# Attention softmax sums inverted in columns and spread by a small product, with the written-out order of all engines laid anew

## What is computed

```python
attn = jax.nn.softmax(sim, axis=-1)
out = jnp.einsum('bhij,bhjd->bhid', attn, v)
out = out.transpose(0, 2, 1, 3).reshape(b, n, h * dh)
return out @ Wout
```

## Time and profile before

| | us |
|---|---|
| median of 3 runs | 3418.23 |
| lowest and highest | 3415.29, 3420.38 |
| the profiled execution's own time | 3428.19 |
| its span | 3425.9 |
| PE busy | 2829.8 (83%) |
| DVE busy | 2313.0 (68%) |
| POOL busy | 1460.9 (43%) |
| ACT busy | 1333.8 (39%) |

### The profile page before, as it was taken

The page is one execution under the profiler, slowest core; times in us unless marked ns, Lnnn a source line. Parts: engine busy times, 40 slices in busy tenths (PEclk is TensorE's granted clock), DMA queues, the critical chain, the costliest instruction groups (busy, mean ns, idle before and its releaser), DMA issues.

```text
span 3425.9 us, 47657 instructions
## 1 busy us (share of the span) xinstructions
PE 2829.8 (83%) x13729; PEld 1419.9 (41%) x13729; DVE 2313.0 (68%) x5792; ACT 1333.8 (39%) x2860; POOL 1460.9 (43%) x1765
## 2 busy tenths in 40 slices
PE   4788787888887877787888888888878788999999
PEld 3333333333333333333333333333333343666666
DVE  6767676768676878686767676767677776444443
ACT  3344434444444444444444343434344433111111
POOL 6354545444555454545454545454545453000000
PEclk8899998989898989898989898989999989999999
DMA  1000000000000000000000000000000010000000
GB/s 42 10 14 6 13 7 13 7 13 7 26 19 13 7 12 8 12 7 12 8 10 10 10 10 10 10 10 10 10 9 7 9 59 1 1 0 16 9 0 25
DMA packets 76232, 41.75 MB, mean 12 GB/s; under 512 B 19024, under 2 KB 74960, under 8 KB 75984
## 3 DMA queue, kind: packets, MB, share of 16 engines
q1 hardware_dynamic: 74448, 34.51, 3.8%
q0 software_dynamic: 1536, 4.20, 0.4%
HBM read 17.55 MB, written 4.19 MB: 6 GB/s over the span
## 4 chain that ended last, share of the span: by engine, by line
PE 39%; DVE 21%; POOL 19%; issue 17%; ACT 4%; POOLq 0%; DMA 0%; ACTq 0%; DVEq 0%
POOL acc L602 12%; PE ps L1188 7%; PE ps L1175 7%; DVE rl L897 5%; DVE ps L854 5%; PE ps L1056 5%; POOL rnorm L583 4%; PE ps L1127 4%; DVE tqk L827 4%; PE ps L1111 3%; DVE tqk L825 3%; PE ps L1084 3%; PE ps L1112 3%; PE ps L1053 2%; ACT probs L689 2%
## 5 line engine op out<-in xcount | busy, mean ns | idle before, releaser
L602 POOL TENSOR_TENSOR acc<-acc,probs 128x512 f32<-128x512 f32 (+4 forms) x944 | 897.0, 950 | 400.0 <-ACT probs L689 326.0
L689 ACT ACTIVATE probs<-ps,btab 128x512 f32<-128x512 f32 (+4 forms) x1408 | 761.9, 589 | 412.9 <-PE ps L1112 264.6
L1127 PE MATMUL ps<-probs,arena 128*64 128x512 f32 (+4 forms) x2816 | 652.4, 541 | 0.0
L854 DVE CUSTOM_DVE_ANT_0 ps<-ps,tab_l 128x512 f32<-128x512 f32 (+1 forms) x896 | 566.3, 672 | 101.4 <-PE ps L1084 98.9
L1111 PE MATMUL ps<-arena 128*128 128x512 f16 (+4 forms) x1408 | 504.4, 360 | 49.1 <-ACT probs L689 47.8
L1084 PE MATMUL ps<-arena 64*128 64x512 f16 (+4 forms) x1408 | 248.8, 346 | 306.4 <-DVE mx L854 300.6
L1112 PE MATMUL ps<-arena 128*128 128x512 f16 (+9 forms) x1408 | 495.8, 354 | 0.0
L580 POOL TENSOR_SCALAR nsq<-ssq 128x4 f32<-128x4 f32 (+1 forms) x272 | 74.6, 274 | 837.5 <-DVE ssq L814 836.8
L645 ACT ACTIVATE sq<-ps 128x256 f32<-128x256 f32 (+1 forms) x272 | 102.3, 376 | 733.2 <-PE ps L1056 731.2
L1056 PE MATMUL ps<-wqkv,xT 128*128 128x256 f32 (+1 forms) x1088 | 366.5, 471 | 0.0
L1084 PEld LDWEIGHTS ps<-arena 64*128 64x128 f16 x1408 | 74.9, 93 | 643.3 <-issue 640.0
(11 more groups left out here) (131 smaller groups left out, 3788.1 us busy)
## 6 DMA issues: line engine op xcount, KB each, us to landing
arena<-arena SPq DMA_DIRECT2D x512, 32.0 KB, 1.9
wqkv<-in_Wkv SPq DMA_DIRECT2D x32, 128.0 KB, 2.5
arena<-in_w SPq DMA_DIRECT2D x2, 2048.0 KB, 11.5
out<-h SPq DMA_DIRECT2D x8, 512.0 KB, 3.0
wqkv<-in_Wq SPq DMA_DIRECT2D x16, 128.0 KB, 2.4
arena<-augs SPq DMA_DIRECT2D x128, 1.0 KB
wo<-in_Wout SPq DMA_DIRECT2D x16, 128.0 KB, 2.2
h<-in_table,idx POOLq DMA_INDIRECT x32, 3.0
```

What stands on the lines that cost most here:

```text
L602: pool.tensor_tensor(a, probs[0:rows, (n - 2) % PB, 0:GW] if first else a, p, ALU.add).then_inc(sum_pool, 1)
L689: nc.scalar.activation(probs[0:rows, n % PB, 0:w], bank(S0 + n % 2)[0:rows, 0:w], ACT.Exp, bias=btab[0:rows, hh, z:z + 1]).then_inc(exp_do ...
L854: nc.vector.tensor_tensor_reduce(bank(A0 + hd)[:, 0:w], bank(A0 + hd)[:, 0:w], tab, 1.0, NEG, ALU.add, ALU.max, mx[:, hd, it, c:c + 1]).th ...
L1127: mm(bank(O0 + o % 2)[DH * hd:DH * hd + DH, c0:GW], vt[t % 2][0:rows, jt, hd, :], probs[0:rows, n % PB, 0:GW - c0], start=(jt == 0), stop= ...
```

## The change

1. The sums are no longer inverted as 128x512. ACT copies them from PSUM to `rl` (`keep_l`). Two DMAs on SP's queue bring one row of 512 for each head into `l_col`, 128 partitions x 4 for each head (`turn_l`). DVE inverts 128x8 (`inv_l`). Two DMAs bring the result back as two rows (`row_l`). PE multiplies these two rows with `of_head`, a 2x128 matrix of ones and zeros, which spreads them over 128x512 in a shared bank (`spread_l`).
2. ACT copies the output from its bank to `otf` (`keep_o`), which frees the bank. DVE multiplies it there with the spread inverses (`divide`). `wout` waits for that.
3. The planned times of nearly all entries are new. `turn_of` keeps entries that use the shared banks at least 0.9 slots apart. The stages of `project` have longer distances for pairs after the first (`LAGS`). `turn_shift` stands 4.4 slots behind `shift`, where it was 0.8. `wout` begins 7.7 slots behind `sums` and its pieces stand at least 2.4 slots apart (it was 2.7 and 2). `sums` stands 4.4 slots behind a group's last block (it was 2.6). `values` and `sum_p` stand later behind their exponentials.
4. `wsum` moves into a part of another buffer, and a wait on `var_ready` is added in `stats_of`.

```diff
+    def turn_of(time):
+        apart = 0.65 if time < 0 else 0.9
+        for other in sorted(taken):
+            if abs(other - time) < apart - 1e-6:
+                time = other + apart
+        taken.append(time)
+        return time
...
+    LAGS = [dict(square=0.4, ssq=1.2, inv=1.9, unit=3.2, high=3.5, low=4.3, turn=4.8),
+            dict(square=0.9, ssq=2.0, inv=2.3, unit=4.2, high=5.0, low=5.8, turn=7.0)]
...
-                at(s0 + 0.9, "shift", t, ig)
-                at(s0 + 1.7, "turn_shift", t, ig)
-                at(s0 + 2.3, "keep_shift", t, ig)
-                at(s0 + 2.4, "put_shift", t, ig)
+                at(s0 + 1.1, "shift", t, ig)
+                s1 = turn_of(s0 + 5.5)
+                at(s1, "turn_shift", t, ig)
+                at(s1 + 0.9, "keep_shift", t, ig)
+                at(s1 + 0.9 + 0.1, "put_shift", t, ig)
...
-            at(t0 + m - 0.9 * (m % 2) + 1.4, "sum_p", t, m)
-            at(t0 + (m | 1) + 1.9, "values", t, m)
+            at(t0 + m - 0.9 * (m % 2) + 1.85, "sum_p", t, m)
+            at(t0 + (m | 1) + 3.5, "values", t, m)
         for ig in range(NG):
-            e0 = t0 + 2 * last_block[ig] + 1
-            at(e0 + 2.6, "sums", t, ig)
-            at(e0 + 3.2, "divide", t, ig)
+            s0 = turn_of(t0 + 2 * last_block[ig] + 1 + 4.4)
+            sums_at[(t, ig)] = s0
+            at(s0, "sums", t, ig)
+            at(s0 + 0.9, "keep_l", t, ig)
+            at(s0 + 0.9 + 0.1, "turn_l", t, ig)
+            at(s0 + 2.9, "inv_l", t, ig)
+            at(s0 + 2.9 + 0.1, "row_l", t, ig)
+            at(s0 + 1.4, "keep_o", t, ig)
+            spread_at.append((turn_of(s0 + 5.0), t, ig))
...
+            def turn_l(t, ig):
+                o = NG * t + ig
+                sp.wait_ge(l_read, o + 1)
+                need(sp, li_out, 32 * o)
+                for hd in range(2):
+                    sp.dma_start(l_col[:, G * hd:G * hd + G], rl[DH * hd:DH * hd + 1, :]).then_inc(l_in, 16)
+
+            def row_l(t, ig):
+                o = NG * t + ig
+                sp.wait_ge(li_ready, o + 1)
+                for hd in range(2):
+                    sp.dma_start(rl[hd:hd + 1, :], l_col[:, G * hd:G * hd + G]).then_inc(li_out, 16)
...
+            def keep_o(t, ig):
+                o = NG * t + ig
+                act.wait_ge(pv_done, PAIR * t + 2 * last_block[ig] + 2)
+                need(act, w_ready, G * (o - 1))
+                nc.scalar.activation(otf[:, o % 2, :], bank(O0 + o % 2), ACT.Copy).then_inc(o_read, 1)
+
+            def keep_l(t, ig):
+                o = NG * t + ig
+                act.wait_ge(l_ready, o + 1)
+                need(act, rl_ready, o)
+                nc.scalar.activation(rl[:, :], shared_of("sums", t, ig)[:, :], ACT.Copy).then_inc(l_read, 1)
...
+            def inv_l(t, ig):
+                o = NG * t + ig
+                dve.wait_ge(l_in, 32 * (o + 1))
+                nc.vector.reciprocal(l_col[:, :], l_col[:, :]).then_inc(li_ready, 1)
+
             def divide(t, ig):
                 o = NG * t + ig
-                dve.wait_ge(l_ready, o + 1)
-                nc.vector.reciprocal(rl[:, :], shared_of("sums", t, ig)[:, :]).then_inc(rl_ready, 1)
                 dve.wait_ge(rl_ready, o + 1)
-                dve.wait_ge(pv_done, PAIR * t + 2 * last_block[ig] + 2)
-                need(dve, w_ready, G * (o - 1))
-                nc.vector.tensor_tensor(otf[:, o % 2, :], bank(O0 + o % 2), rl[:, :], ALU.mult).then_inc(o_read, 1)
+                dve.wait_ge(o_read, o + 1)
+                nc.vector.tensor_tensor(otf[:, o % 2, :], otf[:, o % 2, :], shared_of("spread_l", t, ig)[:, :], ALU.mult).then_inc(o_ready, 1)
...
+            def spread_l(t, ig):
+                o = NG * t + ig
+                pe.wait_ge(li_out, 32 * (o + 1))
+                z = shared_bank("spread_l", t, ig)
+                mm(bank(z)[:, :], of_head[:, :], rl[0:2, :], start=True, stop=True).then_inc(rl_ready, 1)
```

More of the change, by code:

```diff
@@ L194, in lm_tower_kernel @@
     at(-22, "null_unit")
-    at(-20, "null_turn")
-    at(-19, "null_keep")
+    s0 = turn_of(-20)
+    at(s0, "null_turn")
+    at(s0 + 0.6, "null_keep")
     at(-24, "zeros", 1)
-    project(0, -24, 1.6)
-    maxima(0, -14.4, 1.1, lambda g: -24 + 1.6 * (2 * g + 1) + 8)
+    project(0, -24, 1.7)
+    maxima(0, -14.4, 1.2)
+    t0 = max(shifts[(0, ig)] - 2 * blocks.index((ig, 0, 128, 0)) for ig in range(NG))
+    for t in range(PAIRS):
+        attend(t, t0 + PAIR * t)
+        at(t0 + PAIR * t - 40.0 if t else -16, "tables", t)
     for t in range(1, PAIRS):
-        project(t, PAIR * t - 70, 5.0)
-        maxima(t, PAIR * t - 34, 1.85)
+        project(t, t0 + PAIR * t - 74.0, 5.0)
+    for t in range(1, PAIRS):
+        maxima(t, t0 + PAIR * t - 35.0, 1.85)
     for t in range(PAIRS):
-        at(PAIR * t - 38 if t else -16, "tables", t)
-        attend(t, PAIR * t)
+        write(t)
+    for s0, t, ig in spread_at:
+        at(s0, "spread_l", t, ig)
+        at(s0 + 0.9, "divide", t, ig)
     for b in range(1, NB):
         for u in range(T):
-            at(PAIR * (b * NP - 4) + BLKS + 3 + 2.4 * u, "gather", b, u)
-        embed(b, PAIR * (b * NP - 1) - 62, 10)
+            at(t0 + PAIR * (b * NP - 4) + BLKS + 3 + 2.4 * u, "gather", b, u)
+        embed(b, t0 + PAIR * (b * NP - 1) - 63.5, 10)
     for b in range(NB - 1):
-        gate(b, PAIR * (PAIRS - 1) + 2, 4.5)
-    TAIL = PAIR * PAIRS + 14
-    at(PAIR * (PAIRS - 1) + 1, "load_experts")
+        gate(b, t0 + PAIR * (PAIRS - 1) + 1.0, 4.5)
+    at(t0 + PAIR * (PAIRS - 1) + 1, "load_experts")
+    TAIL = wout_from[0] + 1
     gate(NB - 1, TAIL + 1, 4.5)
@@ L217, in lm_tower_kernel @@
     plan.sort()
-    SHARED = ("proj", "sums", "turn_shift", "wout", "turn", "turn_x", "turn_y", "logits", "null_turn")
+    SHARED = ("proj", "sums", "spread_l", "turn_shift", "wout", "turn", "turn_x", "turn_y", "logits", "null_turn")
     shared, nth = {}, {}
@@ L358, in lm_tower_kernel @@
         l_ready = sem("l_ready")
+        l_read = sem("l_read")
+        l_in = sem("l_in")
+        li_ready = sem("li_ready")
+        li_out = sem("li_out")
         rl_ready = sem("rl_ready")
@@ L398, in lm_tower_kernel @@
         NPAR = 8
-        RELEASE = {"proj": p_read, "sums": rl_ready, "turn_shift": aug_kept, "wout": w_added, "turn": ta_done,
+        RELEASE = {"proj": p_read, "sums": l_read, "spread_l": o_ready, "turn_shift": aug_kept, "wout": w_added, "turn": ta_done,
                    "turn_x": xt_out, "turn_y": yt_out, "logits": lg_ready, "null_turn": null_ready}
@@ L492, in _ @@
                     null_v(*which)
+                elif kind == "turn_l":
+                    turn_l(*which)
+                elif kind == "row_l":
+                    row_l(*which)
                 elif kind == "copy_low":
@@ L732, in _ @@
                     tables(*which)
+                elif kind == "keep_l":
+                    keep_l(*which)
+                elif kind == "keep_o":
+                    keep_o(*which)
                 elif kind == "store_x":
@@ L982, in _ @@
                     divide(*which)
+                elif kind == "inv_l":
+                    inv_l(*which)
                 elif kind == "ssq":
@@ L1202, in _ @@
                     turn_shift(*which)
+                elif kind == "spread_l":
+                    spread_l(*which)
                 elif kind == "wout":
```

78 lines of the change are left out of this document (50 added, 28 removed).

## The result

The changed kernel takes 2961.07 us (median of 4 runs, 2958.8 to 2961.99) against 3419.31 for the kernel before: a ratio of 0.866, 95% interval 0.8645 to 0.8675.

What follows compares the result with a forecast made beforehand. PE, busy 83%, was taken as the engine to watch, paced by waits between engines. Terms of -21.8 us a pair over 15 pairs (-327), plus 15 at the ends, took 3428.2 to 3116, median 3106; range 2980 to 3300.

Steps and rivals of the forecast that it cites:

- second rival: Everything closes, PE runs at full clock: 138 us a pair, about 2893 us in all; chance 0.09.
- rule on pieces under 512 bytes: DMA trips: read, modify and write would put landing nearer 4.3 us; the forecast took 1.9 us.
- (a): The large reciprocal leaves DVE, so PE's waits behind it go: -11.9 us a pair, ends 0 and -13.4.
- (b): `turn_shift` stands far behind the unit it needs, so its waits go: -7.0 us a pair, ends 0 and -7.3.
- (c): Other `scores_a` waits, eased by longer distances in `project`: -2 us a pair, ends 0 and -9.2; table waits stay.
- (d): `spread_l`, an fp32 product, is new work for PE: +3.8 us a pair, lower end 2.2.
- (e): ACT's two new 128x512 copies a group fit in its idle time: 0 us a pair, ends 0 and +5.5.
- (f): New waits on the way from `sums` to `spread_l` and its DMA trips: +2.5 us a pair, ends 0 and +8.
- (g): About half of the 14.4 us lost to half clock returns: -7.2 us a pair, ends 0 and -14.4.
- first rival: Only the reciprocal counts and the new order merely moves waits: -8.6 us a pair, 3304 us; chance 0.17.
- own lower end: Total time of about 3020 us, with the clock and other `scores_a` waits near their lower ends.
- The ends: Start and tail of the kernel: +15 us, for later first-pair entries and the last group's DMA trips and spaced products.

Runs made afterwards that it cites:

- e11: The changed kernel with `turn_shift` 0.8 slots behind `shift` again and 0.4 slots more room for the second DMA trip; 2895.2 us.
- e4: The changed kernel with the old distances inside `project` for pairs after the first; 3157.4 us.
- e5: The kernel before with the longer distances inside `project` for pairs after the first, the square keeping 0.5 slots; 3207.0 us.
- e1: The kernel before with the new division path, all other entries at their old planned times; 3339.1 us.
- e2: The changed kernel with the old division (128x512 reciprocal on DVE) in the new order of everything else; 3006.0 us.

## Why the prediction was right and wrong

Right were the bound, the sign, and the reading that PE's 32 us a pair were what could be won. PE's work at full clock was put at 127.3 us, with the product 132.0 by what that measured; e11 shows 131.65. The price of the DMA trips held but for one place: 2.1 us to land, 8.3 us for the way from `sums` to the product against 7.4, and two waits a pair of 2.0 us together, one of them at the boundary of two pairs. The place is the 12.5 us behind the loads of the experts' weights, which no term of the forecast had. The second rival (everything closes) came nearer than the forecast: 140.8 us a pair, it said 138, the forecast 152.

The rule on pieces under 512 bytes in the Trainium skill (DMA: Bandwidth & Descriptors, Specifications) does not show here in the time to landing: pieces of 16 bytes land in 2.1 us, beside 1.9 for pieces of 512, though in transfers of 2 KB against 32. The same page, under "Why small descriptors are slow (HBM only)", exempts transfers within SBUF, and with that the trace agrees.

By the terms, per pair:

| step | forecast | measured |
|---|---|---|
| (a) waits behind reciprocals | -11.9 | -11.9 (gone) |
| (b) `turn_shift` | -7.0 | -7.3 |
| (c) other waits, tables among them | -2.0 | -10.1 |
| (d) spread product | +3.8 | +4.7 |
| (e) ACT's copies | 0 | 0.60 us each, no wait seen |
| (f) new waits | +2.5 | +3.7 |
| (g) clock | -7.2 | about -11 |
| sum | -21.8 | -32, the pair -33.0 |

(The measured terms: `scores_a` 9.2 to 2.0 and the tables 3.1 to 0.2 in (c); what is left of the 5.9 us without `scores_a` and the 0.2 in (f); 14.4 less 3.3 in (g), by which the pair's 134.9 us exceed e11's 131.65.)

**The step that failed is (c)**, "DVE waiting in its order for ACT's squares or POOL's root; the longer distances in `project` give those time. I take -2". Measured were 10.1: 7.2 at `scores_a`, and 2.9 behind the tables, which the forecast had stay. The cause was named and its size guessed from the list of PE's waits, where it shows as 9.2 us. The place to size it was DVE's own list, which I had not put into the rows: 20.0 us in front of the sums of squares alone. e4 and e5 show what the distances of `project` are worth, 196 and 220 us, where the whole change had been put at 312.

**(a) held as a wait, and was nearly all that the division had to give.** The waits behind the reciprocals are gone in e1 and 10.0 us of them are left in e2. Net of the spread product and of the trips, the division alone won 6 to 8 us a pair. The first rival, "only the reciprocal counts", put that at 8.6 and the time at 3304; e1, which is that case made real, measured 3339. The counterpart, that the order does nearly all, was no rival of mine: e2 measured 418 of 458 us.

**(g) was mis-sized with it**, by about 4 us a pair. The clock does not give back a share of the time that waits give back. Over thirteen pairs e5 has more idle time of PE a pair than e1, 23.6 us against 21.9, and yet the higher granted clock, 0.94 against 0.92. The kernel before has 0.90 with 33.1. What decides it is not shown.

The forecast's own lower end, 3020, does not follow from its terms either: (c) and (g) at their ends of -9.2 and -14.4 take another 14.4 us a pair, 216 in all, which gives about 2890. The measured 2961 lies between that and the 3106.

The ends came out near the 15 us forecast, and by luck. Fifteen pairs at 32.5 us are 488, the spans differ by 469.6, so the ends cost 18. In them are the 12.5 us that nobody had priced, 6.3 us that PE waits for the last group's second trip, and a last pair that is 9 us shorter where the forecast had counted nothing.

## What to carry to other kernels

Where engines run in a fixed order, read the waits of the engine that the bound waits for, not only the bound's own: an engine that is 28% idle can hold the bound up, because it stands in front of something not yet due with work queued behind. Before a slow instruction is taken apart, move the stages apart and look again; here the order alone gave 418 us, and the new division 45 on top of it or 85 without it. Distances work together: an edit measured alone (25 us, or a loss of 33) says little of its worth in the set, so take the parts back one at a time from the best version as well. And when short transfers get onto a path, look at what else their queue issues: one set of weight loads ahead of them cost 12.5 us here.

## What was not expected of the hardware

At this density gaps cost more than their length, and not by a fixed rule. Over thirteen pairs PE's idle time in a pair is 7.0 us in the changed kernel and 5.7 in e11, 1.3 less, but the pair is 3.3 us shorter (142.6 and 139.4), since PE's busy time falls by 2.0 with the granted clock. One pair alone says little: these two of the changed kernel follow each other, do the same work with 5.9 us of idle time each, and differ by 4.8 us, all of it clock.

```profile
420.09:562.62 142.53, 136.60 (x739) 60.84 (x739) 109.99 (x311) 80.36 (x174) 85.77 (x101) 0.96 0.06 13
562.62:700.38 137.76, 131.88 (x738) 59.33 (x738) 110.34 (x311) 80.09 (x174) 85.82 (x101) 1.00 0.06 13
```

The product with two rows of input keeps PE busy 0.59 us per instruction for 512 fp32 columns (75.6 / 128), against 0.47 for line 1175 with 128 rows. It stands alone between others, so part of this can be its run-out, and the 75.6 us hold instances at half clock (a pair of them takes 1.12 us in the timeline above, 0.56 each), but the few rows saved nothing.
